# Key sums of the experts: 48 of 64 on GpSimd, 16 on TensorE, with the lane order made anew

## The reference, cut to what matters

```python
q = (xn @ w_q.T).reshape(b, t, H, 2, DK)                       # H = 8 heads
sim1 = jnp.einsum('bthd,hkd->bthk', q[..., 0, :], keys[:, :, 0, :])   # 32 keys
sim2 = jnp.einsum('bthd,hkd->bthk', q[..., 1, :], keys[:, :, 1, :])   # 32 keys
s1, i1 = top_k(sim1, 8); s2, i2 = top_k(sim2, 8)
fs, pk = top_k(s1[..., :, None] + s2[..., None, :], 8)         # 8 of 64 sums
hidden = gelu(xn . expert_down[fi]) * relu(fs)                 # 8 experts of 1024
return einsum('bthk,bthkd->btd', hidden, expert_up[fi])
```

## Time and profile before

| | us |
|---|---|
| median of the runs shown | 1043.43 |
| the profiled execution's own time | 1044.95 |
| its span, first to last instruction | 1043.2 |
| TensorE matmul busy | 794.9 (76%) |
| VectorE busy | 783.7 (75%) |
| ScalarE busy | 665.2 (64%) |
| GpSimd busy | 333.2 (32%) |

### The profile page before, as it was taken

The page is one execution under the profiler, slowest core; times in us unless marked ns, Lnnn a source line. Parts: engine busy times, 40 slices in busy tenths (PEclk is TensorE's granted clock), DMA queues, the critical chain, the costliest instruction groups (busy, mean ns, idle before and its releaser), DMA issues.

```text
span 1043.2 us, 13671 instructions
## 1 busy us (share of the span) xinstructions
PE 794.9 (76%) x4486; PEld 581.0 (56%) x4488; DVE 783.7 (75%) x1651; ACT 665.2 (64%) x1997; POOL 333.2 (32%) x191
## 2 busy tenths in 40 slices
PE   1686496776988798888887739677797889798782
PEld 1566245676556455565664624576655744566561
DVE  1278866998665568989987885699966566998894
ACT  1533559995489397586624446999458959956660
POOL 3033103998366200000014310499847520000000
PEclk9877586999999897979887859689999999989896
DMA  8200002231000000010000000123100000000000
GB/s 242 69 1 0 1 3 73 93 101 62 21 1 1 1 1 1 2 36 1 1 11 11 1 0 12 69 94 100 58 21 1 1 1 0 1 1 1 1 1 21
DMA packets 27248, 29.03 MB, mean 28 GB/s; under 512 B 7220, under 2 KB 17194, under 8 KB 27178
## 3 DMA queue, kind: packets, MB, share of 16 engines
q1 hardware_dynamic: 25208, 26.20, 8.3%
q10 hardware_dynamic: 1970, 1.97, 0.7%
HBM read 26.33 MB, written 1.84 MB: 27 GB/s over the span
## 4 chain that ended last, share of the span: by engine, by line
PE 25%; issue 21%; DVE 20%; POOL 16%; ACT 9%; DMA 4%; POOLq 0%; DVEq 0%; ACTq 0%
POOL mem L1880 11%; ACT mem L1318 5%; DVE mem L1799 5%; DMA mem<-bc_rows 3%; POOL rs L1839 3%; DVE mem L1782 2%; PE ps L1107 2%; PE ps L973 2%; PE ps L934 2%; PE ps L1060 2%; PE ps L1009 1%; POOL mem L1894 1%; PE ps L839 1%; ACT mem L1362 1%; DVE x L1422 1%
## 5 line engine op out<-in xcount | busy, mean ns | idle before, releaser
L1839 POOL TENSOR_TENSOR rs<-ve,minus_half 128x4 f32<-128x4 f32 (+1 forms) x56 | 88.8, 1587 | 510.7 <-DVE ve L1415 440.7
L1880 POOL TENSOR_TENSOR mem<-mem 128x1024 f32<-128x1024 f32 x64 | 166.0, 2621 | 81.3 <-DVE mem L1618 74.6
L1107 PE MATMUL ps<-ident,mem 128*128 128x128 f32 x1024 | 146.4, 297 | 42.1 <-DVE mem L1799 41.4
L1362 ACT ACTIVATE mem<-mem 128x32 f32<-128x32 f32 x768 | 166.9, 311 | 16.9 <-PE ps L1107 16.9
L1799 DVE SCALAR_TENSOR_TENSOR mem<-mem 128x1024 f32<-128x1024 f32 x128 | 160.1, 1277 | 21.8 <-ACT mem L1362 17.9
L1107 PEld LDWEIGHTS ps<-ident,mem 128*128 128x128 f32 x1024 | 125.2, 153 | 85.1 <-DVE mem L1799 62.3
L1138 ACT ACTIVATE mem<-ps 128x1024 f32<-128x1024 f32 (+6 forms) x124 | 91.8, 751 | 118.2 <-PE ps L1060 51.7
L1618 DVE TENSOR_TENSOR_SCAN mem<-mem,ps 128x1024 f32<-128x1024 f32 x64 | 142.4, 2268 | 24.0 <-PE ps L879 24.0
L1318 ACT ACTIVATE mem<-ps,mem,rs 128x77 f32<-128x77 f32 x256 | 101.8, 468 | 18.8 <-DVE mem L1676 18.7
L890 PE MATMUL ps<-ident,mem 128*128 128x128 f32 x512 | 73.6, 291 | 29.0 <-POOL mem L1880 29.0
L879 PE MATMUL ps<-ident,mem 128*128 128x128 f32 x512 | 77.6, 302 | 23.3 <-DVE mem L1618 12.4
(11 more groups left out here) (232 smaller groups left out, 1321.6 us busy)
## 6 DMA issues: line engine op xcount, KB each, us to landing
mem<-bc_rows SPq DMA_DIRECT2D x64, 256.0 KB, 3.2
mem<-in_x_dram SPq DMA_DIRECT2D x4, 256.0 KB, 3.0
mem<-key_rows SPq DMA_DIRECT2D x2, 512.0 KB
out_dram<-x SPq DMA_DIRECT2D x4, 256.0 KB, 2.3
mem<-in_mask_BxSxS_ik_dram SPq DMA_DIRECT2D x4, 154.0 KB, 3.4
mem<-n_L_ffn_expert_down_dram SPq DMA_DIRECT2D x1, 512.0 KB
mem<-in_L_xattn_Wo_dram SPq DMA_DIRECT2D x1, 512.0 KB
mem<-in_L_xattn_Wv_dram ACTq DMA_DIRECT2D x1, 512.0 KB
```

What stands on the lines that cost most here:

```text
L1107: mm = pe.matmul(ps[:, e // 4, (e % 4) * P:(e % 4 + 1) * P], WH[s][:, (k * PH + h) % WB, e * P:(e + 1) * P], ident[:], start=(h == 0 and e ...
L1362: ins = nc.scalar.activation(WH[s][:, n % WB, i * NK:(i + 1) * NK], sims[:, 1, h, :], ACT.Identity, bias=sims[:, 0, h, i:i + 1])
L1839: nc.gpsimd.tensor_tensor(RS[s][0:rows, i * n:(i + 1) * n], VE[s][0:rows, i * n:(i + 1) * n], minus_half[0:rows, 0:n], ALU.pow)\
L1880: nc.gpsimd.tensor_tensor(HC[s][:, n % 2], (HS, TU)[n % 2][s][:], spread(CQ[s][:, n % 2, :], 1, DJ), ALU.mult)\
```

## The change

`SUMS_BY` becomes the same row for all lanes and tiles: six heads G and two heads P. A pass has 48 G and 16 P, no D and no A. A G sum is one GpSimd add of 128 x 1024, with the same operands that the D sum had. It waits for the tile's similarities (`sim_sb`) and, from the fifth head on, for its buffer (`wh_used`), and signals `gsum_ready`, for which line 1799 waits. The generator of ScalarE's own sums goes. The G sums stand in GpSimd's program of the lane behind the second `rsqrt` of the stage (5000) and ahead of the last one, with due times 7 units ahead of the use. The wait for the selection matrix moves from head 0 to the first P head. The semaphore `ssq_done` is folded into `own_done`, with the same waits. All five rows of `LANE_RUNS` are new; lane A now starts first, where lane B did.

```diff
-    SUMS_BY = [('PDADPDPD', 'PDADPDAD'), ('PDADPDAD', 'PDADPDPD')]
+    SUMS_BY = [('GGPGGGPG', 'GGPGGGPG'), ('GGPGGGPG', 'GGPGGGPG')]
...
-            g_sb=8, hw_ready=4, pair_full=18, pair_free=18, aq_ready=4, own_done=26, pn_ready=8, wT_ready=12,
-            asum_ready=6, softplus_step=4, kvar_ready=1, krstd_ready=1, m_sb=2, ssq_done=4,
+            g_sb=8, hw_ready=4, pair_full=16, pair_free=16, aq_ready=4, own_done=14, pn_ready=8, wT_ready=12,
+            gsum_ready=24, softplus_step=4, kvar_ready=1, krstd_ready=1, m_sb=2,
...
         LANE_RUNS = dict(
-            sync=("0 1 1 5 2 1 2 1 1 1 1 1 1 1 1 2 1 1 1 1 1 2 1 1 2 1 5 1 2 1 5 4 3 1 1 1 1 1 1 1 1 1 1 "
+            sync=("1 1 5 2 1 2 3 1 1 1 1 2 1 1 1 1 1 2 1 1 1 1 1 1 1 3 2 1 1 1 5 2 1 2 2 1 2 1 1 1 1 1 1 "
...
-                            if h == 0:
+                            if h == SUMS_BY[s][0].index("P"):
                                 pe.wait_ge(p_toe, 48 + 16 * b)
...
-                            w.next(G("ssq_done", s))
+                            w.reach(G("own_done", s), DJ + k - 1)
...
-                    def own_sums():
...
-                                    for i in range(quarter * NK // 4, (quarter + 1) * NK // 4):
-                                        ins = nc.scalar.activation(WH[s][:, n % WB, i * NK:(i + 1) * NK],
-                                                                   sims[:, 1, h, :], ACT.Identity,
-                                                                   bias=sims[:, 0, h, i:i + 1])
-                                ins.then_inc(G("asum_ready", s), 1)
...
-                    yield from merged(own_sums(), others(), evacuated())
+                    yield from merged(others(), evacuated())
...
-                        nc.vector.tensor_reduce(qv, QSQ[s][:, k % 2], AX.X, ALU.add).then_inc(G("ssq_done", s), 1)
-                        w.next(G("ssq_done", s))
+                        nc.vector.tensor_reduce(qv, QSQ[s][:, k % 2], AX.X, ALU.add).then_inc(G("own_done", s), 1)
+                        w.reach(G("own_done", s), DJ + k + 1)
...
-                                elif SUMS_BY[s][k % 2][h] == "A":
-                                    w.next(G("asum_ready", s))
+                                elif SUMS_BY[s][k % 2][h] == "G":
+                                    w.next(G("gsum_ready", s))
...
-                    for stage in (4060, 5000, 5005 + FIRST + NB * TILE):
+                    for stage in (4060, 5000):
                         yield stage
                         rsqrt(s, P, NB)
+                    for k in range(NB):
+                        for h in range(PH):
+                            if SUMS_BY[s][k % 2][h] == "G":
+                                n = k * PH + h
+                                yield 5000 + max(FIRST - 8, FIRST + TILE * k + HEAD * h - 7)
+                                w.reach(sg["sim_sb"][s], k + 1)
+                                if n >= WB:
+                                    w.reach(sg["wh_used"][s], n - WB + 1)
+                                keys = SIM[s][:, k, :].rearrange("p (h a n) -> p a h n", a=2, h=PH)
+                                nc.gpsimd.tensor_tensor(
+                                    WH[s][:, n % WB, :].rearrange("p (i j) -> p i j", i=NK),
+                                    spread(keys[:, 0, h, :], 2, NK), spread(keys[:, 1, h, :], 1, NK), ALU.add)\
+                                    .then_inc(sg["gsum_ready"][s], 1)
+                    yield 5005 + FIRST + NB * TILE
+                    rsqrt(s, P, NB)
```

More of the change, by code:

```diff
@@ L578, in decoder @@
         LANE_RUNS = dict(
-            sync=("0 1 1 5 2 1 2 1 1 1 1 1 1 1 1 2 1 1 1 1 1 2 1 1 2 1 5 1 2 1 5 4 3 1 1 1 1 1 1 1 1 1 1 "
-                "1 1 1 1 1 1 1 1 1 1 4 2 1"),
-            tensor=("0 3 3 3 1 2 4 3 1 1 1 4 6 5 5 2 1 2 1 1 3 2 1 1 1 1 2 6 2 2 2 2 1 1 2 2 1 2 2 2 1 1 1 "
[7 rows of a table removed]
-            scalar=("0 3 2 1 2 3 3 3 1 1 1 3 5 4 1 1 4 2 1 2 3 5 1 2 4 2 1 1 1 1 1 7 3 1 3 1 3 3 2 2 1 2 1 "
[6 rows of a table removed]
-            vector=("0 3 3 3 1 1 2 2 1 1 1 1 2 2 1 1 1 1 2 4 4 1 1 1 1 1 1 2 3 2 2 5 4 1 1 2 1 2 2 1 1 1 1 "
[8 rows of a table removed]
-            gpsimd=("0 1 1 3 3 2 1 2 3 1 1 1 1 3 1 1 1 1 1 1 1 2 1 1 1 1 1 2 1 1 2 1 2 1 2 1 2 2 2 1 1 3 2 "
-                "2 1 1 2 2 1 1 2 1 1 1 1 1 1 1 4 2 3 3 4 4 1 1 1 1 4 1 1 1 1 1 1 1 1 1 1 1 1 1 1 1 1 1 "
-                "1 1 1 1 1 1 1 4 3 2 2 1 1 2 2 1 1 2 2 1 1 2 1 1 1 1 1 1 1 2 1 1"))
+            sync=("1 1 5 2 1 2 3 1 1 1 1 2 1 1 1 1 1 2 1 1 1 1 1 1 1 3 2 1 1 1 5 2 1 2 2 1 2 1 1 1 1 1 1 "
+                "2 1 2 1 1 1 1 1 1 1 3 2 1"),
+            tensor=("3 3 5 3 1 1 1 1 4 1 1 1 1 4 1 1 3 1 1 5 5 4 1 1 1 2 2 2 6 1 3 1 3 1 1 1 1 1 1 2 1 2 1 "
[7 rows of a table added]
+            scalar=("3 2 1 2 3 3 5 1 2 4 1 2 4 4 1 1 3 4 5 5 4 1 2 1 6 4 1 1 3 3 3 3 2 2 2 3 2 1 1 3 2 3 2 "
[4 rows of a table added]
+            vector=("2 2 1 1 4 2 2 1 1 1 2 2 1 1 2 2 2 1 1 1 1 1 1 3 1 1 3 2 1 3 1 1 1 1 3 4 2 1 3 1 4 1 1 "
[7 rows of a table added]
+            gpsimd=("1 1 3 3 4 4 1 1 1 1 5 1 1 1 1 2 1 1 1 1 1 2 1 1 1 1 1 1 1 1 1 1 1 3 3 2 2 1 1 2 2 1 1 "
[3 rows of a table added]
         def in_turn(program, lane_runs):
@@ L1716, in experts @@
                     ins.then_inc(G("xr_ready", s), 1)
-                    done = [DJ]
+                    done = [DJ + NB]
                     def own(ins):
```

## The result

| | before | after |
|---|---|---|
| median of the runs | 1044.32 us | 1067.15 us (1062.81 to 1068.55) |
| ratio, 95% interval | | 1.0228 [1.0174, 1.0281] |
| span of the profiled execution | 1043.2 us | 1066.8 us |
| TensorE, VectorE busy | 795, 784 us | 782, 841 us |
| ScalarE, GpSimd busy | 665, 333 us | 498, 563 us |

What follows compares the result with a forecast made beforehand. The experts' stage was taken to run at VectorE's pace, TensorE close behind. Turns, uncovered work, start, wait and end gave 178.4 us a pass against 165.2, 26 us more for both: 1070 us, range 1050 to 1085.

Steps and rivals of the forecast that it cites:

- The price of a G: GpSimd's key sum in the experts' stage takes 1.91 us, by line 1894's kind of operand; bounds 1.91 and 2.37.
- The rival at 2.37 us: A G's inner repeat saves nothing, so 20 us come on top in each pass: about 1110 us; chance 0.20.
- The turns: GpSimd's sums and VectorE's two-input arena instructions exclude each other: 79.2 + 73.0 + 5.8 us a pass, 158 us.
- a mean of line 1780 over 2.0 us: Sign of the turns: the threshold, line 1799 before the change, averages over 2.0 us instead of 1.276.
- One-operand work without a G beside it: Of VectorE's 27.4 us a pass beside which a G can run, a third, 9.1 us, stays uncovered; bounds 0 and 27.4.
- Start, wait and end: Stage time without a turn, each pass: 4 us at the start, 4.3 waiting for transposes, 3 at the end.
- The mechanism of the start: Three G of the first lane stand ahead of the other lane's square root; it enters the stage some 6 us later.
- The windows: The experts' stage's two windows come to near 178 us each, against 165.2 on average before.
- all four fractions: Counted shares with bounds: uncovered one-operand work 0 to 27.4 us, transpose wait 0 to 8.5, start 0 to 7, end 0 to 6.
- the turns fit: Rival: all 27.4 us are covered; start, end and wait cost nothing: 158 us a pass, 1029 us; chance 0.21.
- The exclusion does not reach these operands: Faster rival: line 1799 keeps 1.28 us beside a G, TensorE's 134 us sets the pace: 1001 to 1019 us; chance 0.17.

Runs made afterwards that it cites:

- experiment 4: Changed kernel with the two-input threshold of line 1780 replaced by a one-input copying reduction of the same size, GpSimd sums real: 1005.61 us, 0.9616 of the kernel before.
- experiment 5: Changed kernel with the threshold and its small adds, scalar_tensor_tensor and tensor_scalar all replaced by one-operand reductions, GpSimd sums real: 940.13 us, 0.9024 of the kernel before.
- experiment 1: Changed kernel with each GpSimd sum replaced by two memsets of the same buffer, so GpSimd writes but reads nothing: 951.23 us, 0.9126 of the kernel before.
- experiment 6: Changed kernel, whole, with thresholds of the 16 TensorE sums reading the compared operand from PSUM, TensorE and ScalarE orders rewritten: 1045.74 us, 1.0035 of the kernel before.

## Why the prediction was right, point by point

**The price of a G** was forecast as 1.91 us from line 1894, against 2.37 by line 1880. Alone it takes 1.90 to 1.93 us (experiments 4 and 5). The rival at 2.37 us falls.

**The turns.** Laid over each other by start and duration, the intervals in which a G, line 1780 or one of the small lines 1726, 1738 and 1740 is in progress cover 161.0 and 160.3 us of the two windows; the sum had 158.0. What failed was a sign that I named for it, a mean of line 1780 over 2.0 us: it is 1812 ns over the run, since 27 of 64 thresholds a pass waited. A G that begins behind a threshold waits itself, and much of VectorE's waiting fell on the small adds (0.9 us instead of 0.2). Who waits does not change the sum. The Trainium skill (SBUF — State Buffer, Who interferes with whom) says that a VectorE instruction with two SBUF inputs contends with a GpSimd instruction that reads SBUF, and not with one that only writes, and that one with at most one SBUF input does not, outside the modes that use both of VectorE's ports. The prediction left open whether that holds for one tile read twice: it does (2939 against 1258 ns), and experiments 1, 4, 5 and 6 agree with the rule (for the modes, see line 1740 at the end).

**One-operand work without a G beside it:** forecast 9.1 us a pass, measured 11.4 and 11.3 of 26.7 us.

**Start, wait and end:** forecast 4 + 4.3 + 3 = 11.3 us without a turn. Measured: 7.1 and 9.1 us in which VectorE was idle and no G ran, and 6.7 and 3.6 us of VectorE's work on the lane that was still in the attention. The mechanism of the start was only partly right. Four lines of the changed kernel's trace, then the adds of the leading lane's first tile in the kernel before:

```profile
352.59 5.66 POOL L1892 TENSOR_TENSOR mem<-mem 128x1024 f32<-128x1024 f32 x3
353.99 4.31 DVE L1726 TENSOR_TENSOR mem<-mem 128x64 f32<-128x64 f32 x3
362.62 0.17 DVE L1396 TENSOR_SCALAR ve<-mv 128x4 f32<-128x4 f32 x1
362.87 1.98 POOL L1820 TENSOR_TENSOR rs<-ve,minus_half 128x4 f32<-128x4 f32 x1 [4.61 <-DVE ve L1396]
```

```profile
359.44 0.49 DVE L1745 TENSOR_TENSOR mem<-mem 128x64 f32<-128x64 f32 x3
```

The second lane's square root is 6.4 us later than in the earlier trace rows, as forecast, but not because GpSimd was still at its sums: the three G ended at 358.25, and the square root then waited 4.61 us for VectorE. VectorE was late because its small adds had stood behind those same G, 4.31 us instead of 0.49.

The lanes are also further apart. Taken where VectorE ends the layer norm ahead of the stage (line 1403, before 1422), they enter it 24.1 and 20.4 us after each other instead of 15.2 and 10.0. Experiment 5 has the same order without the exclusion, and there it is 19.9 and 16.3 us: so rather more than half of the greater distance is the new order's, the rest the turns'.

**The windows** were to be 178 us and are 186.3 and 184.3. Most of that excess is this distance, for a window counts it from the first lane's start to the second's end. Per lane, from the lane's entry to the end of its last layer norm and averaged over both, the stage grew by 8.8 us in the first pass and 11.3 in the second; with -1.0 us before it, +0.7 between the passes and +3.7 from there to the end of the span, these make up the 23.6 us between the spans, rounding aside. The 3.7 us are nearly all the order's, since experiment 5 has +3.4 there. The forecast had 13.2 + 13.2, and nothing for the other stages. So the total was met by terms of the right kind, each some 2 to 4 us off; that they add up to within 3 us is partly luck.

**The range** of 1050 to 1085 us does not follow from the bounds that it names: with all four fractions at their lower bound the sum gives 1029 us, the time of the rival "the turns fit", and with all at the upper one 1127. The lower end is halfway from the forecast to 1029.

**The rivals.** "The turns fit" falls by the 11 us uncovered and the idle times. "The exclusion does not reach these operands" had its point of decision at thresholds under 1.4 us beside a G; they took up to 2.94. Its price of 1001 to 1019 us was right for thresholds alone (experiment 4, 1005.6 us), and too timid for the whole case that it describes: experiment 5 shows 940 us for that, since TensorE then works without gaps, 125 us a window instead of the 134 that I took from the traces of before, busy for 99% of it, with a granted clock of 1.00 (the upper level throughout), where the windows of before and after had 0.82 to 0.92. That clock is no rival for the loss: it is lower after the change (0.85 and 0.82 against 0.89 and 0.92), but the turns, the one-operand work and VectorE's other work fill the windows but for the 7.1 and 9.1 us above. Only there, or by keeping a G from being ready beside the one-operand work, can a slower TensorE have cost time.

## What to carry to other kernels

Before work goes from VectorE to GpSimd, list what VectorE will run meanwhile: in these runs reductions, MAX8 and operations with an input in PSUM ran beside a GpSimd sum, while operations with two SBUF operands, and a tensor_scalar with one, took turns with it. Where there is little of the first kind to cover it, the moved piece costs its GpSimd time instead of its VectorE time. Short instructions that take turns are the dearest: each can stand behind a whole GpSimd instruction. Read such waits in the spread of an instruction's duration (shortest, median, longest) and not in the idle time before it, and test them by changing the operands, with the order kept.

## What the runs showed of the hardware that was not expected

- A reduction reading 128x1024 from SBUF, 1.209 us, and a G, 1.911 us, ran side by side: none of the 128 and 96 took over 1% longer, and 71 of the 128 had a G beside them (experiment 4). The threshold took 1.275 us with an input in PSUM and up to 2.945 with both in SBUF (experiment 6).
- The tensor_scalar of line 1740, with one tensor operand, is no exception from the turns: it takes 0.171 us in the earlier trace rows, 0.59 in the mean in the second window of the changed kernel, and 0.694 (median, at most 1.043) in experiment 1 with GpSimd's constants, where the two-operand adds took 0.258 at most. So it stands behind GpSimd's writes too. The Trainium skill (SBUF — State Buffer, Who interferes with whom) counts tensor_scalar among those that can take the shared ports in a mode of their own; the trace agrees that it waits, and does not show the mode.
- The exclusion is not symmetric in price: 0.2 us of VectorE's work can wait 1.8 us for a G, while a G waits at most some 1.3 us for a threshold (3.20 against 1.90 us).
